# Attention with FFN on one core: scores of a batch's two 128-token blocks in one PE slot, and a softmax whose operations span both blocks

## Chip, core and metric

The kernel runs on 1 core of one Trainium2 chip. The metric is the device time of one execution in microseconds (us); the median of three executions is given.

## What is computed

x is (32, 256, 256): 32 batches of 256 tokens of 256 features; the context is (32, 77, 256). All in fp32.

```python
x = x + xattn(layernorm(x), ctx, Wq, bq, Wk, bk, Wv, bv, Wo, bo)
x = x + ffn(layernorm(x), ...)

# xattn, 8 heads of 32
logits = einsum('bhqd,bhkd->bhqk', q, k) / sqrt(32) + causal   # (256 tokens, 77 keys) each head
attn = softmax(logits, axis=-1)
out = merge(einsum('bhqk,bhkd->bhqd', attn, v)) @ Wo.T + bo

# ffn: 256 -> 1024 -> 1024 -> 1024 -> 256, weights ternary, a scale per output feature
h = silu(lin(x, w1)) * lin(x, w2)
h = gelu(lin(h, h1)); h = gelu(lin(h, h2))      # exact gelu
return lin(h, w3)
```

The causal mask touches only tokens below 77, so only the first 128-token block of each batch.

## The kernel before

**Tiles.** The 8192 tokens are cut into NT = 16 tiles of 512 tokens: NB = 2 batches, or NQ = 4 blocks of P = 128 tokens (blocks 0 and 1 are batch 0, blocks 2 and 3 batch 1). All weights stay in SBUF. An FFN activation is kept as a high part rounded to fp32r and a low part (the rest), and each product multiplies both, so PE does two matmuls for each 128 x 128 weight block.

**Passes.** A pass handles the FFN of tile f and, in between, the attention of tile f + 1. First comes one pass with the attention of tile 0 alone (list FIRST), in which the weights are also rounded (ROUND on ACT) and checked (CHECK on DVE). Then there are 14 passes in a loop and one behind it with both, then a last one with an FFN alone.

**Order.** There is one hand-written list ORDER of steps. Every engine walks through the same list and issues its own part of each step, in order; semaphores connect the engines. A step's place in the list thus sets its place in the queue of each engine that takes part in it. Letters: L1 n is output block n of the first FFN layer (gate and up product), L2, L3 the two hidden layers, L4 the last; T1, KV, Q the attention's inputs; S n the scores of token block n; EXP n the softmax of block n behind the subtraction; PT n the transposes of the probabilities of block n; PV n probabilities times V of batch n; O the output product.

**PSUM.** ffn_banks has four banks for the FFN, att_banks four for attention. The scores of a block take 154 columns (2 x 77 keys) in each of the four banks of att_banks, one bank for each of four groups of heads.

**The steps around the change.**
- PE, L1 n (L334 to L349): before block n >= 2 it waits for silu and the DVE product of block n - 2. The matmuls themselves are issued at L308.
- PE, S n (L412 to L428): 16 matmuls. S 0 waits for Q, K and V; S 1 and S 3 wait for `masked`, S 2 for `s_copied`, since each overwrites the scores of the block before.
- PE, L2 n (L350 to L367): L2 0 waits k by k for the low parts of L1 (`h_done`); L2 n with n >= 4 waits for the Gelu of n - 4.
- PE, PT n (L429 to L439): waits for `probs_ready` of its block, PT 0 and PT 1 also for `shifted` of all blocks.
- ACT, L1 n: silu of n (L486), then the cast of block n - 1 to its high part (L495); L1E does the last cast. L2 n and L3 n: Gelu twice (L500, L501), once in fp32 and once rounded. S 1 and S 3: copy of the scores from PSUM to `probs` (L520), 616 elements. EXP n (L524): exponential in place, 616 elements.
- DVE, L1 n: product of silu and up (L590), then the low part of block n - 1 (L595). S 0 and S 2: mask added (L625), reading PSUM; then, for each of the four blocks, the maximum of each head (L629) and its subtraction (L631). EXP n (`soften`): sum (L566), reciprocal (L568), product (L570). L2 n: low part of Gelu (L601).

An operation ACT_TABLE_LOAD stands ahead of an ACT operation whose function isn't in the table loaded last (a load ahead of L486, L500 and L524 in each pass). The kernel's text has no line for it; it is put there when the kernel is compiled.

Of the kernel before, what the change touches and what calls it, by code (L numbers as in the profile page):

```python
# [19 lines left out]
ALU = mybir.AluOpType  # L20
ACT = mybir.ActivationFunctionType
AX_X = mybir.AxisListType.X

P = 128
B, TQ, TK, D = 32, 256, 77, 256
H = 8
HD = D // H
HID = 1024
TILE = 512
NB = TILE // TQ  # L30
NT = B // NB
NQ = TILE // P
KD = D // P
KH = HID // P
HG = H // 4
G2 = 2 * TK


def column_of(head):
# [3 lines left out]
SCALE = float(HD) ** -0.5  # L43
# [6 lines left out]

ORDER = [
    ("L1", 0), ("T1", 0), ("L1", 1), ("KV", 0), ("L1", 2), ("Q", 0), ("L1", 3), ("S", 0),
    ("L1", 4), ("L1", 5), ("S", 1), ("L1", 6), ("S", 2), ("L1", 7), ("L1E", 0), ("S", 3),
    ("EXP", 0), ("EXP", 1), ("EXP", 2), ("EXP", 3),
# [10 lines left out]
def steps(ffn, att, nxt):  # L65
# [5 lines left out]

FIRST = [
    ("KV", 0), ("T1", 0), ("ROUND", 0), ("Q", 0), ("CHECK", 0), ("ROUND", 1), ("CHECK", 1), ("ROUND", 2),
    ("S", 0), ("S", 1), ("S", 2), ("S", 3), ("EXP", 0), ("ROUND", 3), ("EXP", 1), ("EXP", 2),
    ("EXP", 3), ("ROUND", 4), ("ROUND", 5), ("CHECK", 2), ("PT", 0), ("PT", 1), ("CHECK", 3), ("PV", 0),
    ("ROUND", 6), ("PT", 2), ("CHECK", 4), ("PT", 3), ("CHECK", 5), ("PV", 1), ("SEED", 0), ("ROUND", 7),
    ("CHECK", 6), ("CHECK", 7), ("O", 0), ("ROUND", 8), ("ROUND", 9), ("LN2S", 0), ("CHECK", 8), ("LN2A", 0),
    ("ROUND", 10), ("CHECK", 9), ("CHECK", 10), ("COUNT", 0), ("T2", 0), ("LN1S", 0), ("LN1A", 0), ("CTX", 0),
# [3 lines left out]
def build_kernel(nc, x, ctx_t, w_att, vectors, w1, w2, h1, h2, w3, out):  # L82
# [4 lines left out]
    with ExitStack() as es:  # L87
# [36 lines left out]
        q_t, _ = put("q_t", [P, HG, TILE], at=b_lo_at + 4096)  # L124
# [16 lines left out]
        k_t, _ = put("k_t", [P, HG, NB * TK])  # L141
# [3 lines left out]
        probs, probs_at = put("probs", [P, NQ, H * TK])  # L145
# [4 lines left out]
        mask, _ = put("mask", [P, TK])  # L150
# [5 lines left out]
        mx, _ = put("mx", [P, NQ, H])  # L156
        total, _ = put("total", [P, NQ, H])
        rtotal, _ = put("rtotal", [P, NQ, H])
# [13 lines left out]
        ab = es.enter_context(nc.psum_tensor("att_banks", [P, 4, 512], F32))  # L172
# [58 lines left out]
        at = 0  # L231
# [68 lines left out]
        def _(pe):  # L300
# [30 lines left out]
            def one_pass(f, a, nxt, general):  # L331
                for step, n in steps(True, a is not None, nxt) if f is not None else FIRST:
# [35 lines left out]
                    if step == "L4":  # L368
# [3 lines left out]
                        for i in range(2):  # L372
                            j = 2 * n + i
# [6 lines left out]
                            else:  # L380
                                mm = product(fb[:, 2 + n, i * D:(i + 1) * D], lambda k: w3_sb[:, k, :], KH, hi, lo,
                                             wait_h, KH * f, w_is_moving=True)
# [4 lines left out]
                    if step == "T1":  # L387
                        pe.wait_ge(ln_ready[0], a + 1)
                        for k in range(KD):
                            for j in range(NQ):  # L390
                                mm = nc.tensor.transpose(ab[:, k, j * P:(j + 1) * P], xln[:, j, k * P:(k + 1) * P], id32[:])  # L391
                        mm.then_inc(t1_ready, 1)
                    if step == "KV":
                        pe.wait_ge(ctx_loaded, 16 * (a + 1))
                        for m in range(HG):
                            for k in range(KD):
                                mm = nc.tensor.matmul(ab[:, 2, m * NB * TK:(m + 1) * NB * TK], wk_sb[:, k, m * P:(m + 1) * P],  # L397
                                                      ctx_sb[:, k, :], start=(k == 0), stop=(k == KD - 1))
# [13 lines left out]
                    if step == "S":  # L412
                        if n == 0:
                            pe.wait_ge(q_done, a + 1)
                            pe.wait_ge(k_done, a + 1)
                            pe.wait_ge(v_done, a + 1)
                        if n == 1 or n == 3:
                            pe.wait_ge(masked, NB * a + n // 2 + 1)
                        if n == 2:
                            pe.wait_ge(s_copied, NB * a + 1)  # L420
                        keys = (n // (TQ // P)) * TK
                        for g in range(HG):
                            at = g * TK
                            for h in range(4):
                                rows = slice(HD * h, HD * (h + 1))
                                mm = nc.tensor.matmul(ab[:, h, at:at + TK], q_t[rows, g, n * P:(n + 1) * P],  # L426
                                                      k_t[rows, g, keys:keys + TK], start=True, stop=True)
                        mm.then_inc(s_ready, 1)  # L428
                    if step == "PT":  # L429
                        pe.wait_ge(probs_ready, NQ * a + n + 1)  # L430
                        if n < 2:
                            pe.wait_ge(shifted, NQ * a + NQ)
                        if n == 3:
                            pe.wait_ge(heads_done, NB * a + 1)
                        pair = (2, 0, 0, 2)[n]
                        for h in range(H):
                            mm = nc.tensor.transpose(ab[0:TK, pair + h // 4, (h % 4) * P:(h % 4 + 1) * P],  # L437
                                                     probs[:, n, column_of(h) * TK:(column_of(h) + 1) * TK], id32[:])
                        mm.then_inc(pt_ready, 1)  # L439
# [38 lines left out]
        def _(act):  # L478
            def one_pass(f, a, nxt):
                for step, n in steps(True, a is not None, nxt) if f is not None else FIRST:  # L480
# [30 lines left out]
                    if step == "Q":  # L511
# [1 line left out]
                        for g in range(HG):  # L513
                            op = nc.scalar.activation(q_t[:, g, :], ab[:, g, :], ACT.Identity, bias=bq_sb[:, g:g + 1])
                        op.then_inc(q_done, 1)
                    if step == "S" and n % (TQ // P) == 1:
                        act.wait_ge(s_ready, NQ * a + n + 1)
                        if n == 3 and not (isinstance(a, int) and a == 0):
                            act.wait_ge(x1_kept, a)
                        nc.scalar.copy(probs[:, n, :].rearrange("p (h g c) -> p h g c", g=HG, h=4),  # L520
                                       ab[:, :, 0:G2].rearrange("p h (g c) -> p h g c", g=HG)).then_inc(s_copied, 1)
                    if step == "EXP":
                        act.wait_ge(shifted, NQ * a + n + 1)
                        nc.scalar.activation(probs[:, n, :], probs[:, n, :], ACT.Exp, scale=SCALE).then_inc(exp_done, 1)  # L524
                    if step == "PT":
                        act.wait_ge(pt_ready, NQ * a + n + 1)
                        q0 = (n % 2) * P
# [15 lines left out]
        def _(dve):  # L543
# [15 lines left out]
                                                 ALU.subtract, ALU.mult)  # L559
                op.then_inc(ln_ready[i], 1)  # L560

            def soften(n, a):

                p = probs[:, n, :].rearrange("p (h c) -> p h c", h=H)
                dve.wait_ge(exp_done, NQ * a + n + 1)
                nc.vector.tensor_reduce(total[:, n, :], p, AX_X, ALU.add).then_inc(sum_done, 1)  # L566
                dve.wait_ge(sum_done, NQ * a + n + 1)
                nc.vector.reciprocal(rtotal[:, n, :], total[:, n, :]).then_inc(rsum_done, 1)  # L568
                dve.wait_ge(rsum_done, NQ * a + n + 1)
                nc.vector.tensor_tensor(p, p, rtotal[:, n, :].unsqueeze(2).broadcast_to([P, H, TK]), ALU.mult)\  # L570
                    .then_inc(probs_ready, 1)

            def one_pass(f, a, nxt):
                for step, n in steps(True, a is not None, nxt) if f is not None else FIRST:
# [34 lines left out]
                    if step == "KV":  # L609
                        dve.wait_ge(v_ready, a + 1)  # L610
                        nc.vector.tensor_tensor(v_sb[:], ab[0:TK, 3, :].rearrange("p (b d) -> p b d", b=NB),
                                                bv_sb[0:TK].unsqueeze(1).broadcast_to([TK, NB, D]), ALU.add).then_inc(v_done, 1)
                    if step == "S":
                        scores = ab[:, :, 0:G2].rearrange("p h (g c) -> p h g c", g=HG)
                        if n % (TQ // P) == 0:
                            dve.wait_ge(s_ready, NQ * a + n + 1)
                        else:
                            dve.wait_ge(s_copied, NB * a + n // 2 + 1)
                        m = mx[:, n, :].rearrange("p (h g) -> p h g", g=HG)
                        p = probs[:, n, :].rearrange("p (h g c) -> p h g c", g=HG, h=4)  # L620
                        if n == 2 and not (isinstance(a, int) and a == 0):
                            dve.wait_ge(x1_kept, a)
                        if n % (TQ // P) == 0:

                            nc.vector.tensor_tensor(p, scores, mask[:].unsqueeze(1).unsqueeze(1).broadcast_to([P, 4, HG, TK]),  # L625
                                                    ALU.add).then_inc(masked, 1)
                            dve.wait_ge(masked, NB * a + n // 2 + 1)
                        scores = p
                        nc.vector.tensor_reduce(m, scores, AX_X, ALU.max).then_inc(max_done, 1)  # L629
                        dve.wait_ge(max_done, NQ * a + n + 1)  # L630
                        nc.vector.tensor_tensor(p, scores, m.unsqueeze(3).broadcast_to([P, 4, HG, TK]), ALU.subtract)\  # L631
                            .then_inc(shifted, 1)
                    if step == "EXP":
                        soften(n, a)
                    if step == "PT":
                        dve.wait_ge(pt_ready, NQ * a + n + 1)
                        q0 = (n % 2) * P
# [118 lines left out]
```

## Time and profile before

| | |
|---|---|
| median of 3 executions | 1691.63 us (1690.36 to 1691.97) |
| the profiled execution | 1691.11 us, span 1689.2 us |
| mean granted clock of PE | 0.985 |
| PE busy | 1635.1 us, 97% |
| DVE busy | 849.1 us, 50% |
| ACT busy | 742.9 us, 44% |
| POOL busy | 131.0 us, 8% |
| chain that ended last | PE 85%, DVE 8%, issue 3%, ACT 1%, POOL 1% |
| DMA over the span | 19 GB/s |

All times of rows are microseconds from the span's start, except means in ns. PE issues a matmul while the one before it is still on its way, so a matmul of 512 columns is shown with 0.39 us though the next starts 0.23 behind it; the pace is read from the starts. ACT and DVE operations overlap by up to 0.1 us where the second doesn't wait for the first.

### The profile page before, as it was taken

The numbers are of one execution on the slowest core, as the hardware profiler recorded it, in microseconds if no ns is written. First come the engines' busy times: TensorE is split into PE (matmuls) and PEld (weight loads), VectorE is DVE, ScalarE is ACT, GpSimd is POOL, SyncE is SP. The second block draws the span as 40 slices with busy tenths as digits, with TensorE's granted clock in tenths as the row PEclk, the third lists the DMA queues.
The fourth block names the chain that finished last, engine by engine and source line by source line (L and its number), as shares of the span: only waits on it lengthen the run. The fifth ranks groups of instructions, "written<-read, shape, count | busy, mean of one in ns | idle before, by whom it ended". The sixth has DMA issues, their size and how long they took to land.

```text
span 1689.2 us, 22426 instructions
## 1 busy us (share of the span) xinstructions
PE 1635.1 (97%) x9090; PEld 1324.4 (78%) x9090; DVE 849.1 (50%) x1453; ACT 742.9 (44%) x1131; POOL 131.0 (8%) x120
## 2 busy tenths in 40 slices
PE   4599999999999999999999999999999999999998
PEld 3378888787887878888787887878888787887887
DVE  6763644737355463644637346463644636346331
ACT  4453543535344353443535345353443535345342
POOL 0300001000000100001000010100001000010000
PEclk7699999999999999999999999999999999999999
DMA  6100000000000000000000000000000000000000
GB/s 275 67 1 13 16 12 16 1 15 12 12 16 12 14 2 12 16 12 16 0 16 12 12 16 12 4 12 12 16 12 16 0 16 12 12 17 1 1 13 13
DMA packets 21094, 32.60 MB, mean 19 GB/s; under 512 B 976, under 2 KB 19408, under 8 KB 19536
## 3 DMA queue, kind: packets, MB, share of 16 engines
q1 hardware_dynamic: 21072, 32.30, 5.5%
q8 instruction: 15, 0.25, 0.1%
q14 instruction: 7, 0.06, 0.0%
HBM read 23.91 MB, written 8.39 MB: 19 GB/s over the span
## 4 chain that ended last, share of the span: by engine, by line
PE 85%; DVE 8%; issue 3%; ACT 1%; POOL 1%; DMA 0%; DVEq 0%; POOLq 0%; SPq 0%; ACTq 0%
PE ffn_banks L308 68%; PE att_banks L437 3%; PE att_banks L409 3%; PE att_banks L454 3%; DVE a_lo L595 2%; PE att_banks L446 2%; DVE a_f L590 2%; PE att_banks L402 2%; DVE mx L629 2%; DVE probs L625 1%; PE att_banks L397 1%; PE att_banks L391 1%; PE att_banks L462 1%; PE att_banks L426 1%; POOL x L688 1%
## 5 line engine op out<-in xcount | busy, mean ns | idle before, releaser
L308 PE MATMUL ffn_banks<-a_hi,h_sb 128*128 128x512 f32 x1024 | 408.4, 399 | 0.0
L308 PE MATMUL ffn_banks<-b_hi,h_sb 128*128 128x512 f32 x1024 | 401.3, 392 | 0.0
L308 PE MATMUL ffn_banks<-a_lo,h_sb 128*128 128x512 f32 x1024 | 400.0, 391 | 0.0
L308 PE MATMUL ffn_banks<-b_lo,h_sb 128*128 128x512 f32 x1024 | 398.6, 389 | 0.0
L601 DVE TENSOR_TENSOR a_lo<-a_f,a_hi 128x512 fp32r<-128x512 f32 x128 | 88.6, 692 | 317.8 <-ACT a_hi L501 317.8
L601 DVE TENSOR_TENSOR b_lo<-b_f,b_hi 128x512 fp32r<-128x512 f32 x128 | 113.9, 909 | 260.1 <-ACT b_hi L501 260.1
L500 ACT ACTIVATE a_f<-ffn_banks,vec 128x512 f32<-128x512 f32 x128 | 88.3, 690 | 354.1 <-PE ffn_banks L308 354.1
L308 PEld LDWEIGHTS ffn_banks<-a_hi,h_sb 128*128 128x128 f32 x1024 | 192.3, 188 | 45.8 <-issue 6.2
L308 PEld LDWEIGHTS ffn_banks<-b_lo,h_sb 128*128 128x128 f32 x1024 | 192.3, 188 | 39.8
L308 PEld LDWEIGHTS ffn_banks<-b_hi,h_sb 128*128 128x128 f32 x1024 | 192.3, 188 | 39.8
L308 PEld LDWEIGHTS ffn_banks<-a_lo,h_sb 128*128 128x128 f32 x1024 | 192.5, 188 | 38.1
L308 PE MATMUL ffn_banks<-ln_hi,w_sb 128*128 128x512 f32 x512 | 216.9, 424 | 4.8 <-issue 4.8
L308 PE MATMUL ffn_banks<-ln_lo,w_sb 128*128 128x512 f32 x512 | 201.9, 394 | 0.0
L500 ACT ACTIVATE b_f<-ffn_banks,vec 128x512 f32<-128x512 f32 x128 | 88.1, 688 | 250.6 <-PE ffn_banks L308 250.4
L486 ACT ACTIVATE a_f<-ffn_banks,vec 128x512 f32<-128x512 f32 x128 | 88.4, 690 | 187.4 <-PE ffn_banks L308 187.4
L590 DVE SCALAR_TENSOR_TENSOR a_f<-ffn_banks,vec,a_f 128x512 f32<-128x512 f32 x128 | 95.7, 748 | 133.7 <-ACT a_f L486 92.0
L308 PE MATMUL ffn_banks<-w_sb,a_hi 128*128 128x256 f32 x512 | 124.9, 286 | 0.4 <-DVE a_lo L601 0.4
L308 PE MATMUL ffn_banks<-w_sb,a_lo 128*128 128x256 f32 x512 | 123.5, 283 | 0.0
L308 PEld LDWEIGHTS ffn_banks<-ln_hi,w_sb 128*128 128x128 f32 x512 | 96.7, 189 | 30.6 <-issue 8.5
L308 PEld LDWEIGHTS ffn_banks<-ln_lo,w_sb 128*128 128x128 f32 x512 | 97.0, 189 | 21.7 <-issue 3.6
L688 POOL TENSOR_TENSOR x<-x_in,vec 128x1024 f32<-128x1024 f32 x16 | 46.5, 2908 | 792.5 <-PE att_banks L437 792.5
L308 PEld LDWEIGHTS ffn_banks<-w_sb,a_hi 128*128 128x128 f32 x512 | 98.2, 192 | 0.7 <-DVE a_lo L601 0.6
(79 smaller groups left out, 1914.2 us busy)
## 6 DMA issues: line engine op xcount, KB each, us to landing
x_in<-in_x SPq DMA_DIRECT2D x16, 512.0 KB, 3.8
stage<-in_h SPq DMA_DIRECT2D x8, 1024.0 KB, 13.3
out<-out_sb SPq DMA_DIRECT2D x16, 512.0 KB, 2.9
stage<-in_w SPq DMA_DIRECT2D x3, 1024.0 KB, 8.4
ctx_sb<-in_ctx_t SPq DMA_DIRECT2D x16, 154.0 KB, 2.2
w_att_sb<-in_w_att SPq DMA_DIRECT2D x1, 1024.0 KB, 5.9
vec<-in_vectors SPq DMA_DIRECT2D x1, 402.0 KB, 6.4
```

Of the source, the lines that this page charges most:

```text
L308: mm = nc.tensor.matmul(psum, left, right, start=(k == 0 and part == 0), stop=(k == rows - 1 and part == 1))
L402: mm = nc.tensor.matmul(ab[0:TK, 3, b * D:(b + 1) * D], ctx_sb[:, k, b * TK:(b + 1) * TK], wv_sb[:, k, :], start=(k == 0), stop=(k == KD - 1))
L409: mm = nc.tensor.matmul(ab[:, m, :], wq_sb[:, k, m * P:(m + 1) * P], ln1_t[:, k, :], start=(k == 0), stop=(k == KD - 1))
L437: mm = nc.tensor.transpose(ab[0:TK, pair + h // 4, (h % 4) * P:(h % 4 + 1) * P], probs[:, n, column_of(h) * TK:(column_of(h) + 1) * TK], i ...
L446: mm = nc.tensor.matmul(ab[HD * h:HD * (h + 1), bank, g * TQ:(g + 1) * TQ], v_sb[:, n, (4 * g + h) * HD:(4 * g + h + 1) * HD], attn_t[:, 4 ...
L454: mm = nc.tensor.matmul(ab[:, 2 + j // 2, (j % 2) * D:(j % 2 + 1) * D], heads_t[:, k, j * P:(j + 1) * P], wo_sb[:, k, :], start=(k == 0), ...
L486: nc.scalar.activation(a_f32[:, n, :], fb[:, 2 * (n % 2), :], ACT.Silu, scale=s1_sb[:, n:n + 1]).then_inc(silu_done, 1)
L500: nc.scalar.activation(f32[:, n, :], fb[:, n % 4, :], ACT.Gelu, scale=scale[:, n:n + 1])
L590: nc.vector.scalar_tensor_tensor(out=a_f32[:, n, :], in0=fb[:, 2 * (n % 2) + 1, :], scalar=s2_sb[:, n:n + 1], in1=a_f32[:, n, :], op0=ALU. ...
L595: nc.vector.tensor_tensor(a_lo[:, m, :], a_f32[:, m, :], a_hi[:, m, :].bitcast(F32), ALU.subtract)\
L601: nc.vector.tensor_tensor(lo[:, n, :], f32[:, n, :], hi[:, n, :].bitcast(F32), ALU.subtract).then_inc(done, 1)
L688: nc.gpsimd.tensor_tensor(x1[:], x_in[:], bo_sb.unsqueeze(1).broadcast_to([P, NQ, D]), ALU.add)\
```

## The change

PE computes the scores of both blocks of a batch in one slot: S n is now batch n, with 32 matmuls, and its scores take 308 columns in each bank. Each of the two S slots is copied out by one ACT operation of 1232 elements. S 1 waits only for the copy of S 0. The mask is then added in SBUF. On DVE, mask, maximum, subtraction and the softmax's tail become steps of their own (MASK n, MAX n, SUB n, SOFT n), for a batch each; all but the mask, which stays at one block, are 1232 elements wide, and so is the exponential EXP n on ACT. The two lists of steps get these steps in new places. In ORDER, EXP 0 now stands ahead of L2 0 and EXP 1 behind it, MASK 1 and MAX 1 are ahead of L2 0, SUB 1 and SOFT 0 behind it, SOFT 1 behind PT 0. PT n waits for the batch's probabilities, and PT 0 also for the second copy.

```diff
 ORDER = [
     ("L1", 0), ("T1", 0), ("L1", 1), ("KV", 0), ("L1", 2), ("Q", 0), ("L1", 3), ("S", 0),
-    ("L1", 4), ("L1", 5), ("S", 1), ("L1", 6), ("S", 2), ("L1", 7), ("L1E", 0), ("S", 3),
-    ("EXP", 0), ("EXP", 1), ("EXP", 2), ("EXP", 3),
-    ("L2", 0), ("L2", 1), ("L2", 2), ("PT", 0), ("L2", 3), ("PT", 1), ("L2", 4), ("PV", 0),
+    ("L1", 4), ("MASK", 0), ("L1", 5), ("MAX", 0), ("S", 1), ("L1", 6), ("SUB", 0), ("L1", 7), ("L1E", 0),
+    ("EXP", 0), ("MASK", 1), ("MAX", 1), ("L2", 0), ("SUB", 1), ("SOFT", 0), ("EXP", 1),
+    ("L2", 1), ("L2", 2), ("PT", 0), ("SOFT", 1), ("L2", 3), ("PT", 1), ("L2", 4), ("PV", 0),
...
 FIRST = [
...
-    ("S", 0), ("S", 1), ("S", 2), ("S", 3), ("EXP", 0), ("ROUND", 3), ("EXP", 1), ("EXP", 2),
-    ("EXP", 3), ("ROUND", 4), ("ROUND", 5), ("CHECK", 2), ("PT", 0), ("PT", 1), ("CHECK", 3), ("PV", 0),
+    ("S", 0), ("MASK", 0), ("MAX", 0), ("SUB", 0), ("S", 1), ("MASK", 1), ("MAX", 1), ("EXP", 0), ("SUB", 1),
+    ("SOFT", 0), ("ROUND", 3), ("EXP", 1), ("SOFT", 1),
+    ("ROUND", 4), ("ROUND", 5), ("CHECK", 2), ("PT", 0), ("PT", 1), ("CHECK", 3), ("PV", 0),
...
 (PE)
-                        if n == 1 or n == 3:
-                            pe.wait_ge(masked, NB * a + n // 2 + 1)
-                        if n == 2:
+                        else:
                             pe.wait_ge(s_copied, NB * a + 1)
-                        keys = (n // (TQ // P)) * TK
-                        for g in range(HG):
-                            at = g * TK
-                            for h in range(4):
+                        for half in range(2):
+                            tokens = slice((2 * n + half) * P, (2 * n + half + 1) * P)
+                            for g in range(HG):
+                                at = half * G2 + g * TK
+                                for h in range(4):
...
                     if step == "PT":
-                        pe.wait_ge(probs_ready, NQ * a + n + 1)
-                        if n < 2:
-                            pe.wait_ge(shifted, NQ * a + NQ)
+                        if n % 2 == 0:
+                            pe.wait_ge(probs_ready, NB * a + n // 2 + 1)
+                        if n == 0:
+                            pe.wait_ge(s_copied, NB * a + NB)
...
 (ACT)
+                        nc.scalar.copy(probs[:, 2 * n:2 * n + 2, :].rearrange("p j (h x) -> p j h x", h=4),
+                                       ab[:, :, 0:2 * G2].rearrange("p h (j x) -> p j h x", j=2)).then_inc(s_copied, 1)
                     if step == "EXP":
-                        act.wait_ge(shifted, NQ * a + n + 1)
-                        nc.scalar.activation(probs[:, n, :], probs[:, n, :], ACT.Exp, scale=SCALE).then_inc(exp_done, 1)
+                        act.wait_ge(shifted, NB * a + n + 1)
+                        nc.scalar.activation(probs[:, 2 * n:2 * n + 2, :], probs[:, 2 * n:2 * n + 2, :],
+                                             ACT.Exp, scale=SCALE).then_inc(exp_done, 1)
...
 (DVE)
+            def heads_of(n):
+                return probs[:, 2 * n:2 * n + 2, :].rearrange("p j (h c) -> p (j h) c", h=H)
...
+                    if step == "MASK":
+                        dve.wait_ge(s_copied, NB * a + n + 1)
+                        scores = probs[:, 2 * n, :].rearrange("p (h c) -> p h c", h=H)
+                        nc.vector.tensor_tensor(scores, scores, mask[:].unsqueeze(1).broadcast_to([P, H, TK]), ALU.add)\
+                            .then_inc(masked, 1)
+                    if step == "MAX":
+                        dve.wait_ge(masked, NB * a + n + 1)
+                        nc.vector.tensor_reduce(per_head(mx, n), heads_of(n), AX_X, ALU.max).then_inc(max_done, 1)
+                    if step == "SUB":
+                        dve.wait_ge(max_done, NB * a + n + 1)
+                        nc.vector.tensor_tensor(heads_of(n), heads_of(n), over_keys(mx, n), ALU.subtract).then_inc(shifted, 1)
+                    if step == "SOFT":
+                        dve.wait_ge(exp_done, NB * a + n + 1)
+                        nc.vector.tensor_reduce(per_head(total, n), heads_of(n), AX_X, ALU.add).then_inc(sum_done, 1)
...
```

## Rows read from the trace of the kernel before

**Rows 1.** The page's first part: busy time and share of the span of each engine.
```profile
PE 1635.1 (97%) x9090; PEld 1324.4 (78%) x9090; DVE 849.1 (50%) x1453; ACT 742.9 (44%) x1131; POOL 131.0 (8%) x120
```

**Rows 2.** Chain of waits, one steady pass: start us, us, what ran or released.
```profile
610.41 0.72 DVE probs L625
...
611.18 0.68 PE att_banks L426 x16
611.86 11.12 PE ffn_banks L308 x48
...
712.79 0.68 PE att_banks L426 x16
```

**Rows 3.** PE in order of time, same pass: start us, us, operation.
```profile
600.84 0.39 PE L308 MATMUL ffn_banks<-ln_lo,w_sb 128*128 128x512 f32 x1
601.16 0.68 PE L426 MATMUL att_banks<-k_t,q_t 32*128 32x77 f32 x16
601.77 0.50 PE L308 MATMUL ffn_banks<-ln_hi,w_sb 128*128 128x512 f32 x1
602.11 0.40 PE L308 MATMUL ffn_banks<-ln_lo,w_sb 128*128 128x512 f32 x1
...
606.28 0.50 PE L308 MATMUL ffn_banks<-ln_hi,w_sb 128*128 128x512 f32 x1
...
608.34 0.68 PE L426 MATMUL att_banks<-k_t,q_t 32*128 32x77 f32 x16
...
610.68 0.40 PE L308 MATMUL ffn_banks<-ln_lo,w_sb 128*128 128x512 f32 x1
...
622.83 1.03 PE L437 MATMUL att_banks<-id,probs 128*77 128x128 f32 x8
```

**Rows 4.** DVE in order of time, same pass.
```profile
606.28 0.74 DVE L590 SCALAR_TENSOR_TENSOR a_f<-ffn_banks,vec,a_f 128x512 f32<-128x512 f32 x1
606.94 0.68 DVE L595 TENSOR_TENSOR a_lo<-a_f,a_hi 128x512 fp32r<-128x512 f32 x1
...
612.70 0.75 DVE L590 SCALAR_TENSOR_TENSOR a_f<-ffn_banks,vec,a_f 128x512 f32<-128x512 f32 x1
...
617.58 0.20 DVE L568 RECIPROCAL rtotal<-total 128x8 f32<-128x8 f32 x1
617.81 0.80 DVE L570 TENSOR_TENSOR probs<-probs,rtotal 128x616 f32<-128x616 f32 x1
```

**Rows 5.** ACT in order of time, same pass.
```profile
613.48 0.62 ACT L495 CAST a_hi<-a_f 128x512 fp32r<-128x512 f32 x1 [2.10 <-DVE a_f L590]
...
614.70 1.28 ACT L524 ACT_TABLE_LOAD   x1
615.99 2.54 ACT L524 ACTIVATE probs<-probs 128x616 f32<-128x616 f32 x4
...
619.85 0.69 ACT L500 ACTIVATE b_f<-ffn_banks,vec 128x512 f32<-128x512 f32 x1
620.44 0.68 ACT L501 ACTIVATE b_hi<-ffn_banks,vec 128x512 fp32r<-128x512 f32 x1
```

**Rows 6.** Groups by line and shape, DVE and ACT: busy us, mean ns, idle before.
```profile
L631 DVE TENSOR_TENSOR probs<-probs,mx 128x616 f32<-128x616 f32 x64 | 51.2, 800 | 2.2
...
L653 DVE TENSOR_TENSOR ln_lo<-att_banks,ln_hi 128x1024 fp32r<-128x1024 f32 x16 | 19.6, 1224 | 3.2 <-ACT ln_hi L536 3.2
...
L520 ACT COPY probs<-att_banks 128x616 f32<-128x616 f32 x32 | 21.5, 673 | 6.2 <-PE att_banks L426 6.2
...
L504 ACT COPY ln_t<-att_banks 128x1024 f32<-128x1024 f32 x16 | 16.1, 1009 | 2.3 <-PE att_banks L391 2.3
```

**Rows 7.** First pass in order of time, DVE and PE.
```profile
39.59 2.28 DVE L583 SCALAR_TENSOR_TENSOR stage<-stage,h_sb 128x2048 f32<-128x2048 f32 x1
...
43.22 1.93 PE L446 MATMUL att_banks<-attn_t,v_sb 77*32 77x256 f32 x16 [5.06 <-DVE attn_t L638]
...
50.76 1.07 PE L446 MATMUL att_banks<-attn_t,v_sb 77*32 77x256 f32 x16 [1.97 <-DVE attn_t L638]
```

More of the change, by code:

```diff
@@ L416, in one_pass @@
                             pe.wait_ge(v_done, a + 1)
-                        if n == 1 or n == 3:
-                            pe.wait_ge(masked, NB * a + n // 2 + 1)
-                        if n == 2:
+                        else:
                             pe.wait_ge(s_copied, NB * a + 1)
-                        keys = (n // (TQ // P)) * TK
-                        for g in range(HG):
-                            at = g * TK
-                            for h in range(4):
-                                rows = slice(HD * h, HD * (h + 1))
-                                mm = nc.tensor.matmul(ab[:, h, at:at + TK], q_t[rows, g, n * P:(n + 1) * P],
-                                                      k_t[rows, g, keys:keys + TK], start=True, stop=True)
+                        for half in range(2):
[3 more added lines that the diff above has]
+                                for h in range(4):
+                                    rows = slice(HD * h, HD * (h + 1))
+                                    mm = nc.tensor.matmul(ab[:, h, at:at + TK], q_t[rows, g, tokens],
+                                                          k_t[rows, g, n * TK:(n + 1) * TK], start=True, stop=True)
                         mm.then_inc(s_ready, 1)
                     if step == "PT":
-                        pe.wait_ge(probs_ready, NQ * a + n + 1)
-                        if n < 2:
-                            pe.wait_ge(shifted, NQ * a + NQ)
+                        if n % 2 == 0:
+                            pe.wait_ge(probs_ready, NB * a + n // 2 + 1)
+                        if n == 0:
+                            pe.wait_ge(s_copied, NB * a + NB)
                         if n == 3:
@@ L515, in one_pass @@
                         op.then_inc(q_done, 1)
-                    if step == "S" and n % (TQ // P) == 1:
-                        act.wait_ge(s_ready, NQ * a + n + 1)
-                        if n == 3 and not (isinstance(a, int) and a == 0):
+                    if step == "S":
+                        act.wait_ge(s_ready, NB * a + n + 1)
+                        if n == 1 and not (isinstance(a, int) and a == 0):
                             act.wait_ge(x1_kept, a)
-                        nc.scalar.copy(probs[:, n, :].rearrange("p (h g c) -> p h g c", g=HG, h=4),
-                                       ab[:, :, 0:G2].rearrange("p h (g c) -> p h g c", g=HG)).then_inc(s_copied, 1)
+                        nc.scalar.copy(probs[:, 2 * n:2 * n + 2, :].rearrange("p j (h x) -> p j h x", h=4),
+                                       ab[:, :, 0:2 * G2].rearrange("p h (j x) -> p j h x", j=2)).then_inc(s_copied, 1)
                     if step == "EXP":
-                        act.wait_ge(shifted, NQ * a + n + 1)
-                        nc.scalar.activation(probs[:, n, :], probs[:, n, :], ACT.Exp, scale=SCALE).then_inc(exp_done, 1)
+                        act.wait_ge(shifted, NB * a + n + 1)
+                        nc.scalar.activation(probs[:, 2 * n:2 * n + 2, :], probs[:, 2 * n:2 * n + 2, :],
+                                             ACT.Exp, scale=SCALE).then_inc(exp_done, 1)
                     if step == "PT":
@@ L560, in ln_apply, with per_head, over_keys @@
                 op.then_inc(ln_ready[i], 1)
[L562 to L571, printed above, removed]
+            def heads_of(n):
+                return probs[:, 2 * n:2 * n + 2, :].rearrange("p j (h c) -> p (j h) c", h=H)
+            def per_head(t, n):
+                return t[:, 2 * n:2 * n + 2, :].rearrange("p j h -> p (j h)")
+            def over_keys(t, n):
+                return per_head(t, n).unsqueeze(2).broadcast_to([P, 2 * H, TK])
             def one_pass(f, a, nxt):
@@ L612, in one_pass @@
                                                 bv_sb[0:TK].unsqueeze(1).broadcast_to([TK, NB, D]), ALU.add).then_inc(v_done, 1)
[L613 to L632, printed above, removed]
@@ L633, in one_pass @@
-                    if step == "EXP":
-                        soften(n, a)
+                    if step == "MASK":
[6 more added lines that the diff above has]
+                        nc.vector.tensor_reduce(per_head(mx, n), heads_of(n), AX_X, ALU.max).then_inc(max_done, 1)
@@ new lines, in one_pass @@
+                    if step == "SUB":
[4 more added lines that the diff above has]
+                        nc.vector.tensor_reduce(per_head(total, n), heads_of(n), AX_X, ALU.add).then_inc(sum_done, 1)
+                        dve.wait_ge(sum_done, NB * a + n + 1)
+                        nc.vector.reciprocal(per_head(rtotal, n), per_head(total, n)).then_inc(rsum_done, 1)
+                        dve.wait_ge(rsum_done, NB * a + n + 1)
+                        nc.vector.tensor_tensor(heads_of(n), heads_of(n), over_keys(rtotal, n), ALU.mult).then_inc(probs_ready, 1)
```

## The prediction

> **What bounds the kernel now.** The first view to read is the busy share of each engine: PE is busy for 97% of the span and DVE for half of it [rows 1]. A reader must not stop there, because a share of 97% says that PE has little to gain, not that nothing can be lost. The second view is therefore the chain that ended last, for one pass of the steady loop. It runs through PE from the fourth score slot to the first transposes of the probabilities without a break: 611.18, then 48 FFN matmuls for 11.12 us [rows 2]. Ahead of that slot it runs through DVE (the mask of token block 2 ends at 611.13). The same slot comes again at 712.79, so a pass lasts 101.61 us [rows 2]. There are 15 passes that hold both an FFN and an attention (14 in the loop, one behind it), one first pass with attention alone, and one last pass with FFN alone, which the change doesn't touch. The third view is the order of time of PE, DVE and ACT around the change, because the question is who is late at the step where PE next needs something.
>
> **Part 1: two score slots fewer on PE.** PE enters a score slot with 0.32 us between the start of the last FFN matmul and the first score matmul (600.84, 601.16), where FFN matmuls follow each other at 0.23 (11.12 us over 48). The 16 score matmuls then take 0.61 (601.16 to 601.77), and the second FFN matmul comes 0.34 behind the first (602.11), again 0.11 more than usual [rows 2, 3]. So a slot costs 0.61 of work and 0.09 + 0.11 = 0.20 for going in and out. The change keeps the 64 score matmuls and has two slots in the place of four: 2 x 0.20 = 0.40 us less. The fourth slot also waits: 610.68 to 611.18 is 0.50, 0.18 more than the 0.32 of the first, for the mask on DVE, since it may not overwrite scores which the mask still reads [rows 2, 3]. In the changed kernel a slot waits for ACT's copy alone. Its second slot comes 0.61 later than the second slot now, which ends at 606.28 [rows 3]: it begins at 606.28, and the copy of the first is done by 603.7 (below). So this wait goes: 0.18 less. Sum: 0.40 + 0.18 = 0.58, call it 0.60. If nothing else were late, the first transposes (PT 0), now at 622.83 [rows 3], would start at 622.23.
>
> **Part 2: wider operations.** On DVE a 616-wide tensor_tensor takes 0.800 us and a 1024-wide one 1.224 [rows 6], so 0.424 for 408 elements, 1.04 ns each; 1232 wide gives 1.224 + 208 x 1.04 ns = 1.44. Two of 616 are 1.60, less 0.08 of overlap between independent neighbours (606.28 + 0.74 = 607.02, but the next starts at 606.94 [rows 4]). I take 1.44 for max, subtraction, sum and product, bounds 1.36 to 1.60. On ACT, 616 elements from PSUM take 0.673 and 1024 take 1.009 [rows 6], so 1232 take 1.009 + 208 x 0.82 ns = 1.18. Four exponentials take 2.54 [rows 5]; half of that is 1.27, and a wide one saves a little: 1.25. DVE has some 1.5 us less work in a pass by this, but it is idle for half the span, so that is worth nothing by itself. ACT copies all four blocks instead of two: 2 x 1.18 - 2 x 0.673 = 1.0 us more. The first copy runs from 602.5 (slot of 1.22 from 601.16, its last matmul's end and the signal 0.1) to 603.7. It pushes the silu of L1 4 by some 0.2. The DVE operation that needs this silu also needs the up product, which begins with L1 4 at 602.38 and is done 1.97 + 0.2 later, 604.55 (these two terms below). The copy costs nothing.
>
> **Part 3: what the new order does to ACT's tables.** This is the part that decides. Now all four exponentials stand together behind L1E and ahead of L2 0. ACT loads the exponential's table (614.70, 1.28 us), runs the four, loads Gelu's and starts Gelu at 619.85 [rows 5]. In the new order EXP 0 stands ahead of L2 0 and EXP 1 behind it, so ACT goes exponential, Gelu, exponential, Gelu: two table loads more in a pass, 2.56 us of ACT. ACT's own time isn't short; the trouble is who waits. On DVE the steps behind L2 0 are SUB 1 and then SOFT 0, and DVE takes them in order. So SOFT 0, which makes the probabilities that PT 0 waits for, stands behind DVE's low part of L2 0, which stands behind the Gelu of L2 0, which stands behind a table load, EXP 0 and another table load. In the kernel before, softmax waits for no Gelu.
>
> I follow this chain through the same pass. The second score slot (606.28) now takes 1.21, so L1 6 starts at 607.49. An L1 step behind a slot lasts 608.34 - 606.28 - 0.09 = 1.97 [rows 3], so it goes on to 609.46. Its last matmul started 0.23 before that and lasts 0.39 [rows 3], so with 0.04 for the signal DVE's product of L1 6 starts at 609.66. DVE then has LO 5 at 610.32 (0.66 on, [rows 4]), SUB 0 at 610.92 and the product of L1 7 at 612.28, against 612.70 now [rows 4]. It ends at 613.03; ACT's cast of L1 7 follows 0.03 later, as now (612.70 + 0.75 = 613.45, 613.48), and ends at 613.68 [rows 4, 5]. Then:
> - load for exp, 1.28, to 614.97; EXP 0, 1.25, to 616.23 (its input SUB 0 is long done)
> - load for Gelu, 1.28, to 617.53; the two Gelus of L2 0, 1.27 (619.85 to 620.44 + 0.68 [rows 5]), to 618.82. PE, in L2 0 from 611.2, is done with it before 616
> - DVE: low part of L2 0 from 618.86; SUB 1 from 619.46; sum of SOFT 0 from 620.82; reciprocal from 622.28; product from 622.51 (0.23 on, as 617.58 to 617.81 [rows 4]), to 623.95. MASK 1 and MAX 1 (2.2 us) fit into the 4.4 us in which DVE waits for Gelu
> - PT 0 at 624.00
>
> PT 0 was due at 622.23, so PE now stands idle for 1.8 us ahead of it, where it had no wait; against the kernel before PT 0 is 624.00 - 622.83 = 1.17 us later. Everything of PE stands behind it in its queue: L2 3 and all that follows. What is late next? ACT: EXP 1 from 620.9 to 622.2, load to 623.5, the Gelus of L2 1 and L2 2 to 626.0. DVE: their low parts to 626.7, its copy of PT 0 to 627.4, SOFT 1 (3.1) to 630.5, the low part of L2 3 and the copy of PT 1 to 631.8. PE: PT 0, L2 3, PT 1 and L2 4 are two times 0.8 and two times 3.7 (11.12 over 3), so PV 0 is due at 633.0 and PT 2, which needs SOFT 1, a slot later. Both are met. The Gelus of L2 1 and L2 2 free the banks that PE takes for L2 5 and L2 6, later still. So one stall in a pass, and from there the pass runs as before. 15 x 1.17 = +17.6 us. Bounds: with the wide operations on DVE at 1.60 the chain gets 4 x 0.16 longer (SUB 0, SUB 1, sum, product), so +1.8 a pass; with the cast of L1 7 and the overlaps better than assumed by 0.6, +0.6 a pass.
>
> A rule bears on this. The Trainium skill (ScalarE: Activation LUTs, "What ACT_TABLE_LOAD costs") gives a switch as a load of about 1.28 us and a drain of about 1.38 us, 2.66 together, and its section on table sets advises to finish all work of one set before switching. The load of 1.28 agrees with the trace; no drain shows, since the load ends at 615.98 and the exponential starts at 615.99 [rows 5]. By the Trainium skill's figure the two loads on the chain would cost an estimated 2.8 us more in a pass.
>
> **Part 4: the first pass.** There no Gelu and no new table stands between, and DVE is the bound: its softmax runs on to the weight check at 39.59, and PE waits 5.06 us for DVE's copies ahead of the first P x V at 43.22 [rows 7]. DVE saves 8 x 0.16 less the overlaps, 2 reciprocals of 0.23 and two short waits for ACT's copies, and starts some 0.7 later because the first mask now waits for a copy. I take -1.5 us, bounds 0 and -2.
>
> **Sum.** The profiled execution took 1691.11 us with a span of 1689.2, within 0.03% of the median 1691.63. 1691.1 + 17.6 - 1.5 = 1707.2 us, +0.95%.
>
> **Rivals.**
> - *The chain is short enough* (faster). If Exp and Gelu could be served without the two loads on the chain, it would end 2.56 us earlier, ahead of 622.23, and only Parts 1 and 4 would remain: 15 x -0.60 - 1.5 = -10.5, 1680.6 us. It decides for faster once the chain loses over 1.3 us, about one load. For it: nothing but that the program that places the loads isn't seen here. Against it: the trace has a load at exactly such a switch [rows 5]. Chance 6%. A chain shorter by just one load, or an equally early cast of L1 7, gives 1688 to 1695: 5%.
> - *PE's clock falls in the new pause.* After 5.06 us of idle time 16 matmuls of P x V took 1.93, at the lower of the two levels (1.2 GHz); after 1.97 us of idle time 16 like them took 1.07, at the upper (2.4 GHz) [rows 7]. A pause of 1.8 is by these rows too short. If it fell and one step of L2 (3.64 us) ran at half speed, it would cost 15 x 3.6 = 54 us more: 1761. Chance 4%.
> - *Each table switch costs a pause of its own* beside the load. If it were as long as the load, 2 x 1.28 more on the chain: 15 x 2.56 = 38, so 1745. Against it speaks the 0.01 us between load and exponential. Chance 3%. This is the drain of the Trainium skill (ScalarE: Activation LUTs), which would make it an estimated 1749.
>
> **How the numbers follow.** The forecast case, slower by the late PT 0, has 82%. Its own range is 15 x 0.6 - 2 = +7 to 15 x 1.8 + 0 = +27, with some room for a longer wait in front of the chain: 1698 to 1722. The rivals outside hold under 2 in 10. A measurement of this kernel can tell about 0.2% from no change. Faster by more: 0.07. Within it: 0.05. Slower: 0.88.
>
> **What would show it.** In the profile after: score matmuls in two groups of 32 with no wait for DVE; 30 table loads for Exp, now one in each of the 15 passes, and 15 more for Gelu; PE idle ahead of PT 0 by 1.8 us, released by DVE's probability product, in each pass; DVE idle for some 2.2 us ahead of the low part of L2 0, on ACT; period 102.8 us. I am wrong if the number of loads stays, if PT 0 waits for nothing, if the wide operations are far from 1.44, or if a second wait (PV 0, PT 2) appears.

## The result

| | before | after |
|---|---|---|
| median | 1691.73 us (4 executions) | 1708.57 us (4 executions, 1706.72 to 1709.30) |
| ratio | | 1.0099, 95% interval 1.0087 to 1.0111 |
| profiled execution | 1691.11 us, span 1689.2 | 1708.57 us, span 1706.5 |
| PE busy | 97% | 95% |
| DVE, ACT busy | 849.1, 742.9 us | 829.9, 794.4 us |

The change made the kernel 1.0% slower. DVE has 19 us less to do and ACT 51.5 us more, and neither tells the reader where 17 us come from. The list of ACT and DVE groups by line and shape shows first that the parts are what they were said to be (line, engine, operation, shapes, count | busy us, mean ns | idle before):

```profile
L501 ACT ACT_TABLE_LOAD x31 | 39.8, 1283 | 0.5
L525 ACT ACTIVATE probs<-probs 128x1232 f32<-128x1232 f32 x32 | 39.5, 1234 | 13.4 <-DVE probs L626 13.3
L525 ACT ACT_TABLE_LOAD x30 | 38.5, 1283 | 0.5
L521 ACT COPY probs<-att_banks 128x1232 f32<-128x1232 f32 x32 | 38.0, 1188 | 22.7 <-PE att_banks L426 22.7
...
L633 DVE TENSOR_TENSOR probs<-probs,rtotal 128x1232 f32<-128x1232 f32 x32 | 46.1, 1442 | 1.1
L626 DVE TENSOR_TENSOR probs<-probs,mx 128x1232 f32<-128x1232 f32 x32 | 45.9, 1435 | 0.1
```

Two more table loads in each of 15 passes (31 + 30, where it was 16 + 15), the wide operations at 1.44 us on DVE, 1.19 and 1.23 on ACT. The second view is that of PE's waits (line waited for by, us in total, times, longest). In the kernel before, no pass of the loop had such a wait at the transposes:

```profile
PE att_banks L438 <- DVE probs L633: 33.4, 16, 8.5
```

One of the 16 is the first pass with 8.5 us; the 15 others share 24.9, so 1.66 each. The chain of waits of one steady pass shows what that wait is made of (start us, us, what ran); it answers to [rows 2 to 5]:

```profile
608.24 1.06 PE att_banks L426 x32
...
619.76 0.62 ACT a_hi L496
620.38 0.02 issue
620.40 1.28 ACT L525
621.68 0.01 issue
621.70 1.24 ACT probs L525
622.93 0.02 issue
622.95 1.28 ACT L501
624.23 0.01 issue
624.25 0.69 ACT b_f L501
624.93 0.59 ACT b_hi L502
625.52 0.02 issue
625.55 0.69 DVE b_lo L604
626.24 1.35 DVE probs L626
627.59 1.36 DVE total L629
628.95 0.02 issue
628.97 0.26 DVE rtotal L631
629.23 0.02 issue
629.26 1.45 DVE probs L633
630.71 0.12 issue
630.83 1.09 PE att_banks L438 x8
...
710.88 1.06 PE att_banks L426 x32
```

In the kernel before, this stretch of the chain was PE alone, 48 matmuls for 11.12 us [rows 2]. Now it leaves PE and goes cast, table load, exponential, table load, two Gelus, low part, SUB 1, three steps of SOFT 0, and back to PE at PT 0. PE's last FFN matmul ahead of PT 0 started at 628.78; without the wait PT 0 would have started 0.23 later, at 629.01 (in e1 below it is 620.40 to 620.63), so it is 1.82 us late. The pass lasts 710.88 - 608.24 = 102.64 us, against 101.61 [rows 2]: +1.03, and 15 x 1.03 = 15.5 of the 17.3 us by which the spans differ. The other 1.8 us lie at the entry into the loop (below).

### The profile page after: what moved, and what is told of

Its sections match the earlier page's. It is cut to its first block, busy times and chain, and to the rows that moved or that the text cites. A ratio compares the mean times of both kernels' runs of the same rounds, so it can differ in the third digit from the quotient of the medians.

```text
span 1706.5 us, 22189 instructions
## 1 busy us (share of the span) xinstructions
PE 1627.1 (95%) x9090; PEld 1322.2 (77%) x9090; DVE 829.9 (49%) x1293; ACT 794.4 (47%) x1129; POOL 131.0 (8%) x120
## 4 chain that ended last, share of the span: by engine, by line
PE 83%; DVE 8%; ACT 5%; issue 2%; POOL 1%; DMA 0%; POOLq 0%; SPq 0%; ACTq 0%; DVEq 0%
PE ffn_banks L309 65%; PE att_banks L438 4%; PE att_banks L410 3%; PE att_banks L455 3%; PE att_banks L447 2%; PE att_banks L426 2%; PE att_banks L403 2%; DVE probs L626 2%; DVE probs L633 1%; DVE total L629 1%; ACT L501 1%; ACT L525 1%; ACT probs L525 1%; PE att_banks L398 1%; DVE a_f L593 1%
## 5 line engine op out<-in xcount | busy, mean ns | idle before, releaser
L438 PE MATMUL att_banks<-id,probs 128*77 128x128 f32 x512 | 71.3, 285 | 33.4 <-DVE probs L633 33.4
```

## Experiments

The ratios are against the kernel before, run on the same chips; its medians there were 1691.5 to 1692.0 us. "e1" and so on are used for short below.

**e1: both exponentials, and all of DVE's softmax, ahead of L2 0.** Everything that the change made wide or merged stays.

```diff
-    ("EXP", 0), ("MASK", 1), ("MAX", 1), ("L2", 0), ("SUB", 1), ("SOFT", 0), ("EXP", 1),
-    ("L2", 1), ("L2", 2), ("PT", 0), ("SOFT", 1), ("L2", 3), ("PT", 1), ("L2", 4), ("PV", 0),
+    ("EXP", 0), ("MASK", 1), ("MAX", 1), ("SUB", 1), ("SOFT", 0), ("EXP", 1), ("SOFT", 1), ("L2", 0),
+    ("L2", 1), ("L2", 2), ("PT", 0), ("L2", 3), ("PT", 1), ("L2", 4), ("PV", 0),
```

> The changed kernel with another order only: SUB 1, SOFT 0, EXP 1 and SOFT 1 all stand ahead of L2 0, so ACT goes exponential, exponential, Gelu (one load of each in a pass, as before the change), and DVE's softmax waits for no Gelu. Theory (PT 0 is late by the chain through two table loads and DVE's low part of L2 0): the probabilities of batch 0 are ready near 1.2 us ahead of PT 0, PE doesn't wait, and the 1.82 us of pause go in each of 15 passes: 1708.6 - 15 x 1.82 = 1681 us, below the kernel before. Rival A (the wide operations or the score slot itself cost the time): stays at 1700 or more. Rival B (SOFT 1 now delays DVE's low parts and its copy of PT 0, so PV 0 is late): between 1685 and 1700, with PE idle ahead of PV 0.

Measured: 1680.77 us (1678.20 to 1681.13, 5 executions), 0.9928 (0.9915 to 0.9942). The chain of its steady pass is PE alone again:

```profile
599.88 1.06 PE att_banks L426 x32
...
605.89 14.90 PE ffn_banks L309 x64
620.79 0.87 PE att_banks L438 x8
...
700.61 1.06 PE att_banks L426 x32
```

The pass lasts 100.73 us. Rival A is out: with the same wide operations and the same slots the kernel is faster than before the change. Rival B doesn't show: PE has no wait ahead of PV 0 in a steady pass. The edit does two things at once, it takes two table loads away and it takes DVE's softmax out from behind Gelu; e2 and e10 part them.

**e2: SOFT 0 ahead of L2 0, all four table loads kept.**

```diff
-    ("EXP", 0), ("MASK", 1), ("MAX", 1), ("L2", 0), ("SUB", 1), ("SOFT", 0), ("EXP", 1),
+    ("EXP", 0), ("MASK", 1), ("MAX", 1), ("SOFT", 0), ("L2", 0), ("SUB", 1), ("EXP", 1),
```

> The changed kernel with SOFT 0 moved ahead of L2 0, nothing else. All four table loads of a pass between L1E and L2 2 stay, and so does ACT's order; only DVE's queue differs, SOFT 0 no longer stands behind the low part of L2 0 and SUB 1. Theory: probabilities are ready 3 us or so before PT 0 is due, no pause, 1708.6 - 15 x 1.82 = 1681 us. Rival (the two added table loads cost by themselves, 2 x 1.28 us in each of 15 passes, or the exponential is the late one): 1700 to 1720.

Measured: 1694.84 us (11 executions), 1.0018 (1.0009 to 1.0027). This is neither. The wait at PT 0 went as the theory said, but another one stands in its place, in PE's waits:

```profile
PE att_banks L447 <- DVE attn_t L637: 18.1, 17, 2.9
```

and in the chain of that pass, from EXP 1 on:

```profile
623.88 1.23 ACT probs L525
625.14 1.28 ACT L501
...
629.50 0.68 DVE attn_t L637
630.18 1.35 DVE total L629
...
633.20 0.68 DVE b_lo L604
633.88 0.61 DVE attn_t L637
634.49 0.14 issue
634.63 1.07 PE att_banks L447 x16
```

PV 0 now comes 0.88 us late, behind a second chain of the same kind: EXP 1, Gelu's table load, the Gelus of L2 1 and L2 2, DVE's copy of PT 0, SOFT 1, and DVE's copy of PT 1. In the changed kernel the same chain is there and is met: its last copy ends at 638.22 (637.54 + 0.68), and PV 0 starts at 640.06. Without the 1.82 us of pause at PT 0, PV 0 would be due at 638.24, and with 0.14 from the copy to PE, as in e2, it could start at 638.36, so the pause hid about 0.1 us of lateness. The other 0.8 are e2's own: with SOFT 0 ahead of SUB 1 in DVE's queue, EXP 1 starts 8.62 us behind the last cast of L1 (623.88 - 615.26) instead of 7.86 (627.62 - 619.76). My expectation looked at one end of the queue only.

**e10: e2 without the exponential's table.** The exponential is replaced by Identity with a scale, so the exponential is left out of the computation.

```diff
-                                             ACT.Exp, scale=SCALE).then_inc(exp_done, 1)
+                                             ACT.Identity, scale=-1e-3).then_inc(exp_done, 1)
```

> The kernel of e2_soft0_first with the exponential replaced by Identity with a scale, so the exponential is left out; order, tiles and waits stay. In e2_soft0_first PE waits 0.88 us ahead of PV 0 in every pass, at the end of a chain SUB 1, EXP 1, table load for Gelu, Gelus of L2 1 and L2 2, DVE's copy of PT 0, SOFT 1, DVE's copy of PT 1. Theory (the same cause as before at another place: the table load behind EXP 1 is on that chain): without it the chain is 1.28 us shorter, the wait goes, 1694.8 - 15 x 1.01 = 1680 us, the time of e1_exp_together. Rival (the wait comes from SOFT 0 ahead of L2 0 on DVE alone, which makes SUB 1 late): a load less changes nothing, 1694.8.

Measured: 1681.17 us (5 executions), 0.9935 (0.9921 to 0.9948); no wait at PV 0 is left in a steady pass. SUB 1 starts 7.15 us behind the last cast of L1 in both kernels (618.37 - 611.22 here, 622.41 - 615.26 in e2), so only the load behind EXP 1 has gone from the chain; the two loads ahead of it in e2 weren't on it. So DVE's order alone doesn't make PV 0 late: it takes the order and the table load together.

**e3: the changed kernel with one load less on the chain.** The same edit as in e10, so the exponential is left out, here with the changed kernel's own order.

> The changed kernel with the exponential replaced by Identity with a scale (same tiles, same waits, same order; the exponential is left out). Identity needs no table of its own, so of the two loads on the chain the first goes, Gelu's stays. Theory: the chain to PT 0 is 1.28 us shorter, the pause falls from 1.82 to 0.5 us, 1708.6 - 15 x 1.28 = 1689 us. If the loads were hidden: no change, 1708. If each switch cost a load and a second pause of similar length: 1681, with no pause left.

Measured: 1688.40 us (9 executions), 0.9973 (0.9964 to 0.9983). In its table of PE's waits the one at the transposes is

```profile
PE att_banks L438 <- DVE probs L633: 12.3, 16, 8.5
```

where the changed kernel has 33.4: 0.25 in a pass instead of 1.66, 1.4 less. A load is 1.28, and without one in between Identity overlaps the cast ahead of it by 0.09 (the operation itself is as long as the exponential, 1233 ns against 1234). So a second pause as long as the load, behind each load, is excluded: one load less would then have taken away the whole of the 1.66.

**e4: one load more.**

```diff
+                        if n == 0 and not (isinstance(a, int) and a == 0):
+                            nc.scalar.activation(junk[:], eps[:], ACT.Silu)
```

> The changed kernel with one Silu of 4 elements behind EXP 0 in each of the 15 passes, on a tile that nobody reads: one more table load (1.28 us) and a small operation (some 0.2) on the chain to PT 0. Theory: the pause ahead of PT 0 grows by 1.5, to 3.3 us, 1708.6 + 15 x 1.5 = 1731 us. If ACT's loads lay in slack: 1708. If the clock of PE falls in a pause of 3.3 us: above 1735, with granted clock below 1.0 behind PT 0.

Measured: 1752.96 us (4 executions), 1.0363 (1.0347 to 1.0379), so +44.4 against the changed kernel, where the longer wait alone explains 22.7 (15 x 1.51). The order of time on PE shows the other half (start us, us, operation, idle before):

```profile
645.65 1.54 PE L439 MATMUL att_banks<-id,probs 128*77 128x128 f32 x8 [3.17 <-DVE probs L636]
...
649.12 0.59 PE L310 MATMUL ffn_banks<-a_lo,h_sb 128*128 128x512 f32 x1
649.55 0.40 PE L310 MATMUL ffn_banks<-a_hi,h_sb 128*128 128x512 f32 x1
```

The pause grew from 1.66 to 3.17 us, as expected. Behind it the FFN matmuls follow each other at 0.43 us instead of 0.23, until 649.5: the granted clock has fallen to the lower of its two levels (1.2 GHz). The view of busy time by stretch has the mean granted clock at 0.77 from 644 to 648 and 0.81 from 648 to 652, and 1.00 around them. In the changed kernel, after 1.66 us of idle time, the clock stays at 1.00 in all three such stretches from 624 to 636. The third outcome in the expectation is thus what happened: 1.5 us of load (with its small operation) and some 1.5 us of clock in each pass.

**e5: e1 with each score slot cut in two on PE.**

```diff
+                            if i == 1 and a is not None and n == 4:
+                                scores_of(0, 1).then_inc(s_ready, 1)
+                            if i == 1 and a is not None and n == 5:
+                                pe.wait_ge(s_copied, NB * a + 1)
+                                scores_of(1, 0)
```

> The kernel of e1_exp_together with each score slot cut in two again on PE alone, in the passes that hold an FFN: the second block's 16 matmuls of batch 0 come between gate and up product of L1 4, the first block's of batch 1 between gate and up product of L1 5. Copies, widths and the rest stay. It measures what a slot costs beyond its matmuls. By the prediction 0.20 us each, so 2 x 0.20 x 15 = +6 us against e1_exp_together. By the trace of the changed kernel, where 32 matmuls take 1.07 us and 16 took 0.61, 0.35 each: +10.5 us. If slots are free: 0.

Measured: 1690.90 us (11 executions), 0.9998 (0.9989 to 1.0007): +10.1 against e1.

```profile
601.96 0.61 PE att_banks L338 x16
602.57 1.14 PE ffn_banks L309 x4
603.72 0.61 PE att_banks L338 x16
...
703.46 0.61 PE att_banks L338 x16
```

A pass lasts 101.50 us, 0.77 more than in e1 for two slots more. A slot costs 0.38 us beside its matmuls, not 0.20. (15 x 0.77 would be 11.6 us in all; the medians differ by 10.1, and the rest isn't traced.)

**e6: only the table switches, in the kernel before.**

```diff
-    ("EXP", 0), ("EXP", 1), ("EXP", 2), ("EXP", 3),
-    ("L2", 0), ("L2", 1), ("L2", 2), ("PT", 0), ("L2", 3), ("PT", 1), ("L2", 4), ("PV", 0),
+    ("EXP", 0), ("EXP", 1), ("L2", 0), ("EXP", 2), ("EXP", 3),
+    ("L2", 1), ("L2", 2), ("PT", 0), ("L2", 3), ("PT", 1), ("L2", 4), ("PV", 0),
```

> The kernel before with EXP 2 and EXP 3 moved behind L2 0: four table loads in a pass there instead of two, the softmax of blocks 0 and 1 still ahead of L2 0 on DVE. Theory (a table load costs only where PE waits for the chain that it is on): PT 0 needs blocks 0 alone and is in time, 1691.7 us within 2. Rival (loads cost by themselves): 15 x 2.56 = +38, 1730.

Measured: 1691.73 us (11 executions), 1.0001 (0.9992 to 1.0010), with 30 loads for the exponential and 31 for Gelu, as in the changed kernel:

```profile
L524 ACT ACT_TABLE_LOAD x30 | 38.5, 1283 | 0.6
```

The same 30 added loads cost nothing here: the table of PE's waits has no wait in a steady pass, so no chain that holds them is late for PE. It is the chain, not the load.

**e7, e8, e9: the entry into the loop.** At the entry of the changed kernel's loop PE stands still a second time, which it doesn't in the kernel before (order of time; "issue" is a wait for nothing that the profile shows):

```profile
75.15 0.79 PE L309 MATMUL ffn_banks<-ln_hi,w_sb 128*128 128x512 f32 x1 [5.15 <-issue]
75.74 0.63 PE L309 MATMUL ffn_banks<-ln_lo,w_sb 128*128 128x512 f32 x1
78.10 0.80 PE L309 MATMUL ffn_banks<-ln_hi,w_sb 128*128 128x512 f32 x1 [1.73 <-issue]
```

Between 75 and 77 the DMA view has one transfer, of the instruction queue q8, and none of any other; narrower windows put it at 75.5 to 75.75, ahead of the gap, which begins at 76.37. PE's part of the program has fewer waits and may thus have another length, so I moved the code, with instructions in the branch that isn't run, and changed nothing that is executed. e7 is e1 with 16 of them, e8 the changed kernel with 16, e9 is e1 with 96.

```diff
             with pe.If(count > 0):
                 whole_program(pe, lambda f, a, nxt: one_pass(f, a, nxt, True))
+                for _ in range(16):
+                    nc.tensor.drain()
```

> The kernel of e1_exp_together with 16 more PE instructions at the end of the branch that is never run here (the one for weights that aren't exact), so that the code of the loop that does run lies 16 instructions later. Nothing that is executed differs. In the changed kernel and in e1 PE stands idle for 1.7 to 2.0 us after the first two FFN matmuls of the loop, while a block of instructions is fetched, and its clock then rises later than in the kernel before. Theory (the place of the code decides on that pause): the pause goes, and with it some 3 us: 1677.5 us. Rival (it comes from the first pass's new order): 1680.8, pause unchanged.

> The changed kernel with the same 16 instructions in the branch that is never run. By the theory of e7_shifted_code 1708.6 - 3.7 = 1705 us (pause 1.93, later rise of the clock 1.84); by its rival 1708.6. Were it 1705, the first pass's gain of the prediction would be there, and the 15 passes cost 15 x 1.03.

> As e7_shifted_code with 96 instructions instead of 16: if the pause comes where a fetched block ends, it should be absent or lie at another place of the first L1 steps; 1677 to 1681 us.

Measured: e7 1677.37 us (5 executions), 0.9915 (0.9902 to 0.9929); e8 1705.21 (5), 1.0082 (1.0068 to 1.0096); e9 1677.24 (4), 0.9917 (0.9902 to 0.9933). The second pause is gone in all three. In e8:

```profile
75.16 0.79 PE L309 MATMUL ffn_banks<-ln_hi,w_sb 128*128 128x512 f32 x1 [4.85 <-issue]
75.75 0.63 PE L309 MATMUL ffn_banks<-ln_lo,w_sb 128*128 128x512 f32 x1
```

The medians differ by 3.4 us in both pairs; against the kernel before that was run beside each, the difference is 3.1 (16.84 and 13.75) and 2.9 (11.21 and 14.09). So some 3 of the changed kernel's 16.8 us come from where its code lies, and not from what it does. Why is open. That a block of instructions ends just behind the second matmul would fit, but e8 has the same transfer of q8, at 76.0 to 76.25, and no pause; only that moving the code removes the pause is shown.

## Why the prediction was right

**The late PT 0 (Part 3)** was right in its mechanism and in size. From the start of the first score slot to PT 0 it gave 624.00 - 601.16 = 22.84 us; the trace has 630.83 - 608.17 = 22.66 (608.17 is the slot's start in order of time, 608.24 in the chain). The terms: load 1.28, EXP 0 1.24 (1.25), load 1.28, Gelus 1.27, low part to PT 0 5.28 (5.14). The pause is 1.82 us (1.8). DVE idles 2.26 us ahead of the low part of L2 0 (2.2). e1, e3 and e4 take the wait away, shorten it by one load and lengthen it by one; e6 shows that the loads cost PE nothing where it doesn't wait for them.

**The wide operations (Part 2)**: 1.44 and 1.18 were measured as 1.43 to 1.44 and 1.19. They are worth nothing in a steady pass, as said: of the 0.88 us that a pass of e1 is shorter than before, two slots at 0.38 (e5) and the mask's wait of 0.18 already make 0.94.

**The two slots less (Part 1)** were right in sign and too small. The term was 0.60 us in a pass. The pass of e1, which has no wait, is 101.61 - 100.73 = 0.88 shorter than before. The step that failed is that I took the 0.61 us of a slot with 16 matmuls for pure work. A slot of 32 takes 1.06, so the second 16 take 0.45, and 0.16 of the 0.61 belong to the slot. e5 has it from the other side, 0.38 for a slot. With this term 0.28 larger and the pause 0.05 longer than forecast (1.82 against 624.00 - 622.23 = 1.77), the pass should have lost 0.94 us. It lost 1.03 where the forecast had 1.17, so 15 x 0.14 = 2.1 us less; of the other 0.09, 0.06 are PT 0 itself, whose next FFN matmul comes 0.85 behind its start and in e1 0.79.

**What is late next**: the prediction said that PV 0 is met at 633.0 by a copy that ends at 631.8, with PT 0 at 624.0. That held: 1.8 us lie between the copy and PV 0 in the trace (1.2 forecast). The slack is there because PE was late itself. It was given in the presence of the stall, which is right for the forecast and of little use for a repair: without the pause nothing would be left of it, and e2, whose order makes EXP 1 another 0.76 late, had PV 0 late by 0.88.

**The rival on the clock** was rightly held unlikely for a pause of 1.8 us, and too dear: it put 3.6 us on a fall in each pass, and in e4 a fall cost some 1.5.

**The first pass (Part 4)** was wrong in its sum. Up to the first FFN matmul of the loop it came out near: 75.15 against 77.02, -1.87 (-1.5). That is in part luck. DVE's own gain is 1.33 (the weight check starts at 38.26, before at 39.59 [rows 7]); another 0.86 came from the first P x V, which ran 1.07 us at the upper level of the clock behind 2.91 us of idle time, where before it ran 1.93 at the lower behind 5.06 [rows 7]. Then a second pause of PE and a later rise of the clock took 3.8 us, a term that the prediction doesn't have. In the chains of waits the first product of step KV in the loop stands so in the kernel before, the changed kernel and e8:

```profile
83.30 1.05 PE att_banks L397 x8
...
85.20 1.05 PE att_banks L398 x8
...
82.56 1.05 PE att_banks L398 x8
```

So +1.9 in the changed kernel and -0.7 in e8, which has no second pause. The granted clock rises at about 80.2 in the kernel before, 80.7 in e8 and 84.0 in the changed kernel (by its mean from 80 to 82: 0.95, 0.82 and 0.50), so even in e8 more than half of the earlier start is lost. The sum of 1707.2 came within 1.4 us of the median by luck, because two errors offset each other: 2.1 us too much in the passes, 3.3 too little ahead of them (+1.8 where -1.5 was forecast).

**The drain** that the Trainium skill (ScalarE: Activation LUTs, "What ACT_TABLE_LOAD costs") puts beside the load, about 1.38 us, doesn't show here. Of the five loads in a pass of the changed kernel, those whose operation waits for nothing else are followed by it at once (0.01 to 0.02 us), and e3, with one load less, left 0.25 us of the pause of 1.66, where a load with a drain would have been more than the whole pause. The advice of the Trainium skill (ScalarE: Activation LUTs, "Rules for kernel authors") to finish one table set before the next fits e1, 27.8 us faster than the changed kernel, of which e2 has 13.7 by DVE's order alone, with all loads kept. e6 sets a limit to it: where the chain isn't late, the switches are free.

**Best version**: e7, with the change's wide operations and merged slots, both exponentials ahead of L2 0 and the shifted code: 1677.4 us, 0.85% under the kernel before. Some 3 us of this hang on where the code lies.

## What to carry to other kernels

Where an engine is busy for 97%, as here, an operation moved on another engine matters by who stands behind it in the queues: write down when the busy engine next needs something, and add up the chain to it, table loads included. When a step is split between two uses of ACT's tables, count the loads on that chain, not those in total; the same 30 loads cost nothing in one order and 1.8 us of pause a pass in another. And before a repair is trusted, add up the chain to the next step too, without the stall and in the repair's own order.

## What the runs showed of the hardware

- PE's granted clock stayed at its upper level through 1.66 us of idle time in each pass of the changed kernel and fell to the lower after 3.17 us in e4. The fall cost another 1.5 us or so in a pass, as much as the load that caused it. In the first pass of the changed kernel it was at the upper level after 2.91 us of idle time.
- A group of 16 small score matmuls (77 columns) among FFN matmuls costs 0.61 us and a group of 32 costs 1.06; with the gaps around it, a group costs 0.38 us beside its matmuls (e5).
- The place of code that is not executed changed the time by some 3 us (1680.8 to 1677.4, and 1708.6 to 1705.2; 2.9 and 3.1 against the kernel before run beside each), by a pause of PE behind its second matmul in the loop, 1.2 us after the first one's start.
- An ACT table load that stands ahead of an operation which waits runs during the wait: in the changed kernel the second load for the exponential starts right behind the Gelus of L2 0 at 625.53 and is done 1.28 later, while EXP 1, which it is for, waits for DVE and starts at 627.62.
